# First layer's experts taken half by half, with each half's norm and query product moved among other work

## The chip, the cores and the metric

The kernel runs on one core of one Trainium2 chip. A core has a matrix engine (TensorE, PE in the profile), a vector engine (VectorE, DVE), an activation engine (ScalarE, ACT), a general engine (GpSimd, POOL) and a sync engine (SyncE, SP), which here only issues DMAs. Each runs its own instruction stream in order; they meet at semaphores. The metric is the time of one execution on the device, in microseconds (us); less is better.

## What is computed

Four layers on x, 8 batches of 128 tokens with 128 features, all in float32. Every layer is a cross attention and a mixture of experts (or feed forward), each behind a layer norm. Cut to what the change touches:

```python
x = x + tanh(g_xattn[0]) * L0_xattn(layernorm(x), ctx)
x = x + tanh(g_ffn[0]) * L0_ffn(layernorm(x))      # 8 experts, top 2, + 1 shared of double width
x = x + tanh(g_xattn[1]) * L1_xattn(layernorm(x), ctx, ctx, mask, Wq, bq)
x = x + tanh(g_ffn[1]) * L1_ffn(layernorm(x))      # own norm with gain; 8 experts, some "specialists"
# ... layers 2 and 3

def L0_ffn(x):      # w: softmax of x @ gate_w.T, top 2, normalised
    y = sum(w[:, e] * ((silu(x @ wg[e]) * (x @ wu[e])) @ wd[e]) for e in range(8))
    return y + (silu(x @ swg) * (x @ swu)) @ swd

def L1_xattn(q, k, v, mask, Wq, bq):      # 16 heads of 8, 77 keys per batch
    s = heads(q @ Wq.T + bq) @ heads(k).T / sqrt(8)
    return softmax(where(mask == 0, min, s)) @ heads(v)
```

## The kernel before

The 1024 tokens are two halves of 512 (HALF), four batches each (TH = 4). X is the residual stream with tokens in partitions, XN its normed form, XT (with its parts XTh and XTl) the normed form turned, with features in partitions. PS[0] to PS[7] are the eight PSUM banks. A float32 product is made of three matmuls (`mm3`) on a high and a low part of each operand. So every weight is split first: a "strip" is a cast on DVE to WH (`high_part`, L936) and then a subtraction on POOL to WL (`low_part`, L607). Weights arrive by DMA in RAW.

*The plan.* `plan()` writes the order of a mixture's steps by hand; PE, ACT, DVE and POOL each walk the same list ORDER[layer] in `mixture` and do their part of each step. For the first layer there are five units (E0P = 5): unit 0 is the shared expert, units 1 to 4 are pairs of experts. A step n of the list interleaves (`weave`) three things for successive pairs (unit, half): "gate_up" of x[n] (eight products into banks, Silu on ACT, product with the routing weight on DVE into SN), "turn0" of x[n-1] (SN turned, split in hidden parts H1h/H1l or H2h/H2l) and "down0" of x[n-2], which adds to bank PS[4 + half]. In before x runs (unit 0, half 0), (unit 0, half 1), (unit 1, half 0) and so on, so both halves' sums are complete only at the end. The strips of the next unit come with every second step. "route" parts 0 to 4 are the routing on DVE.

*Between experts and attention.* ACT copies the sums out of PS[4] and PS[5] into XT; PE turns them back (`turn_back`, L1538); DVE adds them to X (`summed`, L1103) and takes moments (`stats`, L891 to L900); POOL takes the power -1/2 (`rstd`, L600); DVE scales (`scaled`, L910); PE turns XN (`turn`, L1386); ACT copies to XT; PE multiplies with Wq; ACT adds the bias and writes the queries QT. POOL builds the key blocks BDK (`head_keys`, L640), two batches ahead; BDK lies over SN. Sixteen `keep_clock` matmuls on constants fill PE meanwhile.

*The attention.* `attention` runs on four engines, 32 iterations of one group of four heads (NG = 4 groups per batch), with lags: in iteration i PE makes the scores of group i in PS[i % 3] (L1366, BDK and a mask matmul MB), the transposes of group i-3 in PS[3 + g % 3] (L1563), and the values of group i-5 in PS[6 + batch % 2]. DVE takes the maximum of i (L1144) and subtracts it for i-1 (L1152), ACT the exponential (L769). The transposed groups are copied out by ACT, every fourth by DVE (L1157). For a finished batch DVE weighs the result (L1163 to L1177), for the first four of them followed by a "bias row" (three instructions for the specialists' biases). From iteration 22 on DVE also does half 0's two norms of the next mixture (`first_half_normed`). Half 1's follow behind the attention, and the step "second" turns them and computes the router's logits.

*The second mixture* starts with the four "up" products of expert 0, half 0, then "second", then four "spec0" tiles of 13 matmuls, each with its norm, woven with half 1's "up".

## Time and profile before

| | |
|---|---|
| median of three runs | 790.73 us (788.05 to 791.43) |
| span of the profiled execution | 791.2 us |
| PE busy | 700.5 us, 89% |
| DVE busy | 553.0 us, 70% |
| mean granted clock of PE | 0.922 |
| first layer's experts, on PE | 34.4 to 115.8 us |
| second attention, on PE | 131.5 to 200 us |

The span is the time from the first to the last instruction of one execution; durations of instructions come from that execution. A granted clock of 1.00 is 2.4 GHz, of 0.5 is 1.2 GHz; a stretch in between shows both. A busy PE may be doing keep-clock matmuls, which compute nothing. Rows give the start and the duration in us, and in brackets how long the engine was idle before and what released it.

### The profile page before, as it was taken

Reading aid. Unit: us, or ns where it says so; the run is one execution under the profiler, and the core shown is the slowest. Engines: PE = TensorE matmul, PEld = TensorE weight load, DVE = VectorE, ACT = ScalarE, POOL = GpSimd, SP = SyncE. Lnnn points to the kernel's source line nnn. Section 1 sums busy time; section 2 is a strip of 40 time slices with the busy share of each in tenths; the row PEclk is TensorE's granted clock in tenths of the full one; section 3 lists DMA queues with packets and bytes.
Section 4 is the critical chain, followed back from the end, with each engine's and each line's share of the span. In section 5 each row is a group of like instructions: output and inputs, shape, how many; then the busy total and the mean of one; then the engine's idle time right before and its main releaser. Section 6 shows DMA issues by size and latency. Waiting matters only on the chain.

```text
span 791.2 us, 10027 instructions
## 1 busy us (share of the span) xinstructions
PE 700.5 (89%) x3468; PEld 547.8 (69%) x3475; DVE 553.0 (70%) x1242; ACT 367.5 (46%) x647; POOL 209.9 (27%) x193
## 2 busy tenths in 40 slices
PE   5989997999898998797999797993759999789997
PEld 2779983889666766675777586771546888567775
DVE  4688766788578585656667735769874554588996
ACT  2334442434435737455275464721214442486673
POOL 5113107322132041124424311143002220214431
PEclk9589997999799999999999989986879999799999
DMA  5102003000001010202010200030000000001000
GB/s 134 39 27 58 2 4 114 31 1 1 1 14 67 3 38 1 68 0 80 14 68 14 66 1 0 1 97 0 1 0 1 1 1 1 27 27 28 1 1 27
DMA packets 27361, 20.97 MB, mean 27 GB/s; under 512 B 5409, under 2 KB 22571, under 8 KB 27311
## 3 DMA queue, kind: packets, MB, share of 16 engines
q1 hardware_dynamic: 26591, 20.29, 8.7%
q8 instruction: 28, 0.46, 0.3%
q14 instruction: 22, 0.18, 0.1%
q10 hardware_dynamic: 720, 0.04, 0.1%
HBM read 19.80 MB, written 0.52 MB: 26 GB/s over the span
## 4 chain that ended last, share of the span: by engine, by line
PE 70%; DVE 17%; issue 4%; ACT 4%; POOL 3%; DMA 1%; ACTq 0%; DVEq 0%; POOLq 0%
PE PS L1366 61%; PE PS L1563 4%; DVE H2l L1082 2%; PE PS L1448 2%; POOL WL L607 2%; ACT H1h L752 1%; DVE SN L1038 1%; PE PS L1499 1%; ACT G L750 1%; DVE WH L936 1%; DVE XN L910 1%; PE PS L1386 1%; DMA GW<-in_L_gate_T 1%; DVE ST L891 1%; POOL RSTD L617 1%
## 5 line engine op out<-in xcount | busy, mean ns | idle before, releaser
L607 POOL TENSOR_TENSOR WL<-RAW,WH 128x512 fp32r<-128x512 f32 (+2 forms) x76 | 95.4, 1272 | 186.9 <-DVE WH L936 186.9
L1082 DVE TENSOR_TENSOR H2l<-G,H2h 128x512 fp32r<-128x512 f32 x104 | 84.0, 822 | 59.7 <-ACT H2h L752 58.7
L1082 DVE TENSOR_TENSOR H1l<-G,H1h 128x512 fp32r<-128x512 f32 x80 | 63.3, 800 | 28.9 <-ACT H1h L752 28.1
L1366 PE MATMUL PS<-H1h,WH 128*128 128x512 f32 x146 | 60.9, 417 | 8.0 <-DVE H1l L1082 8.0
L750 ACT ACTIVATE G<-PS,UB 128x512 f32<-128x512 f32 x64 | 44.8, 700 | 42.4 <-PE PS L1366 38.1
L1366 PE MATMUL PS<-XTh,WH 128*128 128x512 f32 x128 | 55.3, 432 | 9.8 <-POOL WL L607 5.3
L600 POOL TENSOR_TENSOR RSTD<-VE,MHALF 128x4 f32<-128x4 f32 x18 | 19.3, 1072 | 166.5 <-DVE VE L900 166.5
L1366 PEld LDWEIGHTS PS<-V,ATT 77*128 77x128 f32 x512 | 62.5, 192 | 0.6
L625 POOL TENSOR_TENSOR XT<-XT,YW 128x512 f32<-128x512 f32 x24 | 34.8, 1448 | 106.0 <-DVE YW L1017 106.0
L769 ACT ACTIVATE ATT<-ATT 128x308 f32<-128x308 f32 x64 | 29.4, 460 | 71.3 <-DVE ATT L1152 71.0
L1366 PE MATMUL PS<-V,ATT 77*128 77x9 f32 x512 | 61.3, 247 | 0.0
L1144 DVE TENSOR_REDUCE MX<-PS 128x4 f32<-128x308 f32 x64 | 30.5, 477 | 43.6 <-PE PS L1366 42.9
L1366 PE MATMUL PS<-H1l,WH 128*128 128x512 f32 x146 | 58.6, 401 | 0.0
L1366 PE MATMUL PS<-H1h,WL 128*128 128x512 f32 x146 | 58.4, 400 | 0.0
L1366 PE MATMUL PS<-H2h,WH 128*128 128x512 f32 (+1 forms) x108 | 50.6, 469 | 5.6 <-issue 2.0
L1366 PE MATMUL PS<-XTl,WH 128*128 128x512 f32 x128 | 54.0, 422 | 0.0
L685 ACT ACTIVATE ATT<-PS 77x512 f32<-77x512 f32 (+5 forms) x76 | 38.2, 517 | 33.6 <-PE PS L1734 17.0
L1366 PE MATMUL PS<-XTh,WL 128*128 128x512 f32 x128 | 53.8, 420 | 0.0
L1366 PE MATMUL PS<-BDK,ATT 128*128 128x308 f32 x128 | 49.1, 466 | 1.6 <-issue 1.6
L750 ACT ACTIVATE G<-PS,FB 128x512 f32<-128x512 f32 x64 | 43.3, 698 | 13.9 <-PE PS L1366 13.8
L1366 PE MATMUL PS<-H2h,WL 128*128 128x512 f32 (+1 forms) x108 | 44.0, 408 | 0.0
L1366 PE MATMUL PS<-H2l,WH 128*128 128x512 f32 (+1 forms) x108 | 44.0, 407 | 0.0
(242 smaller groups left out, 1677.8 us busy)
## 6 DMA issues: line engine op xcount, KB each, us to landing
RAW<-in_L_ffn_spec_W SPq DMA_DIRECT2D x4, 1024.0 KB, 5.6
RAW<-in_L_ffn_w SPq DMA_DIRECT2D x16, 256.0 KB, 3.0
RAW<-in_L_ffn_up_W SPq DMA_DIRECT2D x8, 256.0 KB, 2.7
RAW<-in_L_ffn_down_W SPq DMA_DIRECT2D x8, 256.0 KB, 3.6
RAW<-in_L_ffn_spec1a_W SPq DMA_DIRECT2D x2, 512.0 KB, 4.3
RAW<-in_L_ffn_spec1b_W SPq DMA_DIRECT2D x2, 512.0 KB, 5.2
RAW<-in_L_ffn_wg SPq DMA_DIRECT2D x4, 176.0 KB, 2.7
RAW<-in_L_ffn_wu SPq DMA_DIRECT2D x4, 176.0 KB, 2.7
```

Source lines behind the costliest of these rows:

```text
L600: g.tensor_tensor(RSTD[:, c], VE[:, c], MHALF[:, c], ALU.pow).then_inc(rstd_ready, 1)
L607: g.tensor_tensor(lo, RAW[0:r["rows"], r["raw"] + s["c0"]:r["raw"] + s["c1"]], hi.bitcast(fp32), ALU.subtract).then_inc(lo_done, 1)
L617: g.tensor_tensor(RSTD[:, i:i + 1], VE[:, i:i + 1], MHALF[:, 0:1], ALU.pow).then_inc(trstd_ready, 1)
L625: g.tensor_tensor(y, y, YW[:, (d % 2) * HALF:(d % 2 + 1) * HALF], ALU.add).then_inc(y_added, 1)
L685: return s.activation(o, i, ACT.Copy)
L750: last = s.activation(G[:, k % 4, :], bank[:, :], func, bias=bias, scale=scale)
L769: s.activation(group(PB, g), group(SUB, g), ACT.Exp, scale=scale).then_inc(exp_done, 1)
L1082: v.tensor_tensor(lo, full, hi.bitcast(fp32), ALU.subtract).then_inc(split_done, 1)
L1144: v.tensor_reduce(MX[:, (g % 4) * GH:(g % 4 + 1) * GH], bank(g), AX.X, ALU.max).then_inc(max_done, 1)
L1366: return t_.matmul(o, l, r, start=start, stop=stop)
L1448: last = t_.transpose(o[0:rows, t * S:(t + 1) * S], SN[:, h, at:at + rows], ident[:, :])
L1563: last = t_.transpose(PS[3 + g % 3][0:KC, m * S:(m + 1) * S], group(PB, g)[:, m * KC:(m + 1) * KC], ident[:, :])
```

## The change

1. In the first layer x becomes (0,0), (0,1), then units 1 to 4 of half 0, then units 1 to 4 of half 1. Strips of units 1 to 4 come in steps 0 to 3, one unit per step. SN is used by step (slot n % 2), no longer by half.
2. Half 0's sum is complete at the end of step 7. Its copy, turning back, sum, moments, scaling, turn, Wq product and bias are steps of their own (the kinds in HELD) between the pieces of steps 7 to 10, in bank PS[4].
3. Half 1's same chain stands inside the second attention: PE's parts in iterations 1, 9 and 12 (`second_half`), DVE's in 2, 3, 4 and 6 (`second_half_normed`), ACT's in 8 and 10, in bank PS[5]. The attention's transposes therefore have two banks instead of three, in both attentions that use the function. QT, SUB and PB lie elsewhere, and the queries of half 1 are waited for at batch 4.
4. The six strips before the second mixture (`prepare(1)`) move on DVE from ahead of the attention to its iterations 10 to 15, on POOL from ahead of the third key block to behind the fifth. POOL's first key block waits for the last hidden split.
5. Half 0's turn for the second mixture stands in the attention's iteration 34. Half 1's two norms stand between the "up" splits, and two specialist tiles ahead of "second". Ring banks 6 and 7 wait for the attention's last outputs. The fourth layer's mixture turns half 1 in PS[5] too.
6. The turning back, the 16 keep-clock matmuls and the turns ahead of the attention are gone.

```diff
-    x = [(p, h) for p in range(E0P) for h in range(2)]
+    x = [(0, 0), (0, 1)] + [(p, h) for h in range(2) for p in range(1, E0P)]
...
-        more = strips(n // 2 + 1) if n % 2 == 0 and n // 2 + 1 < E0P else []
+        more = strips(n + 1) if n + 1 < E0P else []
...
+        elif n == E0P + 2:
+            order[0] += weave(a, b, c) + chain("y_copy")
+        elif n == E0P + 3:
+            u = weave(a, b, c)
+            order[0] += u[:3] + chain("y_back") + u[3:6] + chain("y_sum") + u[6:8] + chain("y_stats") + u[8:]
+        elif n == E0P + 4:
+            u = weave(a, b, c)
+            order[0] += u[:4] + chain("y_scale") + u[4:8] + chain("x_turn", "x_copy") + u[8:]
+        elif n == E0P + 5:
+            u = weave(a, b, c)
+            order[0] += u[:2] + chain("q_up", "q_copy") + u[2:]
...
-    o += up(0, 0) + second
+    u, s = up(0, 0), group("spec0", 1, 0, 0, TH)
+    o += u[0:1] + chain("late_scale") + u[1:2] + chain("late_stats") + u[2:4] + chain("late_norm") + s[0:2] + second
...
-            rstd(4, 5)
+            rstd(4)
+            pool.wait_ge(split_done, LAST0["hid"])
             head_keys(1, CT, range(2))
+            rstd(5)
+            head_keys(1, CT, range(2, TH + 1))
             prepare(1)
-            head_keys(1, CT, range(2, B - 1))
+            head_keys(1, CT, range(TH + 1, B - 1))
...
+                    if not first and i == 8:
+                        turned(2, halves=(1,), bank=PS[5])
+                    if not first and i == 10:
+                        queries(1, PS[5])
+                    if not first and i == B * NG + 1:
+                        turned(3, split=True, affine=True, halves=(0,), bank=PS[5])
...
+            def second_half_normed(i):
+
+                if i == 2:
+                    y0_summed(1, PS[5])
+                elif i == 3:
+                    moments(1, X)
+                elif i == 4:
+                    variances(2, 1)
+                elif i == 6:
+                    scaled(2, 1, X, XN)
+                elif 10 <= i < 10 + len(BEFORE[1]):
+                    high_part(BEFORE[1][i - 10])
...
-            norm(2, X, XN, summed(0))
-            prepare(1)
             attention(0, 1)
 
+            low_of_xt(1, (0,))
             stats(3, 1, X)
-            low_of_xt(1, (0,))
-            scaled(3, 1, X, XN)
-            dve.wait_ge(xn_ready, TH * (NORM_STEP[3, 1] + 1))
-            stats(4, 1, XN)
-            scaled(4, 1, XN, XM)
-            now(stream_plus_norm(1))
             mixture(1, 1)
...
-                    if g - g0 >= 3:
-                        pe.wait_ge(*copied_out(g - 3))
+                    if g - g0 >= 2:
+                        pe.wait_ge(*copied_out(g - 2))
                     for m in range(GH):
-                        last = t_.transpose(PS[3 + g % 3][0:KC, m * S:(m + 1) * S],
+                        last = t_.transpose(PS[3 + g % 2][0:KC, m * S:(m + 1) * S],
...
+            def second_half(i):
+
+                if i == 1:
+                    y0_back(1, PS[5])
+                elif i == 9:
+                    turn(2, *normed(2, XN), halves=(1,), bank=PS[5])
+                elif i == 12:
+                    queries(1, PS[5])
+                elif i == B * NG + 2:
+                    turn(3, *normed(4, XM), halves=(0,), bank=PS[5])
...
-            pe.wait_ge(split_done, LAST0["hid"])
-            turn_back(0)
-
-            keep_clock(16)
-            turn(2, *normed(2, XN))
```

PE from the last expert product to the first scores of the attention, before (XT,WQ are the query products, BDK the key blocks):

```order
L1366 MATMUL PS<-H1l,WH 128x512
L1366 MATMUL PS<-H1h,WL 128x512
L1538 MATMUL PS<-ident,XT 128x128 x8
L1366 MATMUL PS<-MB,identb 128x512 x16
L1386 MATMUL PS<-ident,XN 128x128 x8
L1366 MATMUL PS<-XT,WQ 128x512 x2
L1366 MATMUL PS<-BDK,ATT 128x308
```

and the same place of the changed kernel:

```order
L1422 MATMUL PS<-H1l,WH 128x512
L1422 MATMUL PS<-H1h,WL 128x512
L1422 MATMUL PS<-BDK,ATT 128x308
L1422 MATMUL PS<-MB,identb 128x308
L1422 MATMUL PS<-MB,identb 128x512 x3
L1451 MATMUL PS<-ident,XT 128x128 x4
L1422 MATMUL PS<-BDK,ATT 128x308
```

The scores now follow the last product directly, and half 1 is turned back behind the first of them.

POOL from the last strips of the first mixture through the attention, before (RSTD is the power, BDK a key block, WL a low part):

```order
L607 TENSOR_TENSOR WL<-RAW,WH 96x128
L600 TENSOR_TENSOR RSTD<-VE,MHALF 128x4 x2
L640 TENSOR_TENSOR BDK<-CT,HM 128x1232 x2
L607 TENSOR_TENSOR WL<-RAW,WH 128x512 x6
L640 TENSOR_TENSOR BDK<-CT,HM 128x1232 x5
```

and of the changed kernel:

```order
L622 TENSOR_TENSOR WL<-RAW,WH 96x128
L615 TENSOR_TENSOR RSTD<-VE,MHALF 128x4
L655 TENSOR_TENSOR BDK<-CT,HM 128x1232 x2
L615 TENSOR_TENSOR RSTD<-VE,MHALF 128x4
L655 TENSOR_TENSOR BDK<-CT,HM 128x1232 x3
L622 TENSOR_TENSOR WL<-RAW,WH 128x512 x6
L655 TENSOR_TENSOR BDK<-CT,HM 128x1232 x2
```

The six low parts moved from ahead of the third key block to behind the fifth, and half 1's power stands behind the second.

DVE behind the attention, changed kernel (XTl the low part of half 0, L922 to L931 moments of half 1, L1113 splits of the "up" results, L941 scalings, L1061 a tile's moments):

```order
L957 TENSOR_TENSOR XTl<-XT,XTh 128x512
L922 BN_STATS ST<-X 128x6 x4
L928 BN_AGGR MV<-ST 128x2 x4
L931 TENSOR_SCALAR VE<-MV 128x4
L1113 TENSOR_TENSOR H1l<-G,H1h 128x512
L941 TENSOR_SCALAR XN<-X,MV,RSTD 128x128 x4
L1113 TENSOR_TENSOR H1l<-G,H1h 128x512
L922 BN_STATS ST<-XN 128x6 x4
L928 BN_AGGR MV<-ST 128x2 x4
L931 TENSOR_SCALAR VE<-MV 128x4
L1113 TENSOR_TENSOR H1l<-G,H1h 128x512 x2
L941 TENSOR_SCALAR XM<-XN,MV,RSTD 128x128 x4
```

In before XTl stood behind the first moments, and the four splits in one row behind the whole norm chain.

## Rows read from the trace of the kernel before

**Rows 1.** Page: busy time of each engine; shares of the last chain.
```profile
PE 700.5 (89%) x3468; PEld 547.8 (69%) x3475; DVE 553.0 (70%) x1242; ACT 367.5 (46%) x647; POOL 209.9 (27%) x193
PE 70%; DVE 17%; issue 4%; ACT 4%; POOL 3%; DMA 1%; ACTq 0%; DVEq 0%; POOLq 0%
```
**Rows 2.** Stretches: length; busy PE, PEld, DVE, ACT, POOL; clock; DMA.
```profile
83.30:98.00 14.70, 14.70 (x94) 13.74 (x93) 11.75 (x27) 7.09 (x14) 3.05 (x4) 1.00 0.00 0
98.00:105.20 7.20, 7.20 (x48) 6.72 (x46) 4.74 (x12) 3.55 (x7) 0.00 (x0) 1.00 0.01 2
116.00:132.00 16.00, 10.60 (x35) 4.76 (x34) 12.15 (x34) 3.56 (x6) 11.32 (x7) 0.78 0.31 98
140.00:160.00 20.00, 20.00 (x153) 17.70 (x152) 14.24 (x36) 8.45 (x18) 4.92 (x3) 1.00 0.02 5
210.00:214.00 4.00, 4.00 (x13) 3.25 (x14) 2.35 (x4) 0.56 (x1) 0.00 (x0) 0.52 0.00 0
```
**Rows 3.** Timeline, experts to attention: start, duration, engine, line, instruction [idle before, releaser].
```profile
112.96 0.69 DVE L1075 TENSOR_TENSOR H1l<-PS,H1h 96x512 fp32r<-96x512 f32 x1 [0.28 <-ACT H1h L685]
...
115.40 0.39 PE L1366 MATMUL PS<-H1h,WL 96*128 96x512 f32 x1
...
118.39 0.69 DVE L1103 TENSOR_TENSOR X<-PS,X 128x512 f32<-128x512 f32 x1
...
120.51 6.24 DVE L910 TENSOR_SCALAR XN<-X,MV,RSTD 128x128 f32<-128x128 f32 x8
...
121.69 4.46 POOL L640 TENSOR_TENSOR BDK<-CT,HM 128x1232 f32<-128x1232 f32 x2
...
131.52 1.36 PE L1366 MATMUL PS<-BDK,ATT 128*128 128x308 f32 x2 [0.82 <-issue]
```
**Rows 4.** Timeline of PE, second attention: iterations 2 and 3, and later transposes.
```profile
135.93 0.68 PE L1366 MATMUL PS<-BDK,ATT 128*128 128x308 f32 x2
...
137.23 0.68 PE L1366 MATMUL PS<-BDK,ATT 128*128 128x308 f32 x2
...
161.92 0.60 PE L1563 MATMUL PS<-ident,ATT 128*77 128x128 f32 x4
```
**Rows 5.** PE: four transposes and what follows; last chain: two query products.
```profile
61.15 0.60 PE L1448 MATMUL PS<-ident,SN 128*128 128x128 f32 x4
61.50 0.41 PE L1366 MATMUL PS<-WH,XTh 128*128 128x352 f32 x1
...
597.03 1.93 PE PS L1366 x4
```
**Rows 6.** Slack in the attention; duration ns min/median/max of three kinds; POOL's low parts.
```profile
152.70 0.46 ACT L769 ACTIVATE ATT<-ATT 128x308 f32<-128x308 f32 x1 [2.65 <-DVE ATT L1152]
...
153.97 0.60 PE L1563 MATMUL PS<-ident,ATT 128*77 128x128 f32 x4
...
L910 DVE TENSOR_SCALAR XN<-X,MV,RSTD x8: 335/341/2286, 120.5 to 126.4; 128x128 f32<-128x128 f32 x8
...
L1167 DVE TENSOR_SCALAR RC<-RC,ANY x8: 233/233/1431, 149.3 to 199.8; 128x16 f32<-128x16 f32 x8
...
L936 DVE CAST WH<-RAW x22: 329/416/1032, 43.8 to 128.3; 128x352 fp32r<-128x352 f32 x8, 128x512 fp32r<-128x512 f32 x6, 128x256 fp32r<-128x256 f32 x4, 96x128 fp32r<-96x128 f32 x4
...
L607 POOL TENSOR_TENSOR WL<-RAW,WH 128x512 fp32r<-128x512 f32 (+2 forms) x76 | 95.4, 1272 | 186.9 <-DVE WH L936 186.9
```
**Rows 7.** Timeline: a copy by DVE, and the transposes two groups on.
```profile
190.87 0.68 DVE L1157 COPY ATT<-PS 77x512 f32<-77x512 f32 x1
...
192.94 0.64 PE L1563 MATMUL PS<-ident,ATT 128*77 128x128 f32 x4
```
**Rows 8.** Timeline of PE behind the attention: first "up", turn, second tile.
```profile
202.92 0.47 PE L1366 MATMUL PS<-XTh,WH 128*128 128x512 f32 x1 [2.60 <-DVE XTl L926]
...
207.84 1.10 PE L1386 MATMUL PS<-ident,XM 128*128 128x128 f32 x4 [0.34 <-DVE XM L910]
...
217.40 0.50 PE L1366 MATMUL PS<-ROWr,onesr 33*128 33x512 f32 x1
```

More of the change, by code:

```diff
@@ L360, in program @@
         K3T = ATT3[:, 2048:2048 + B * KC]
-        U0T = ATT[0:R0, 0:T]
+        U0T = ATT2[0:R0, 2048:2048 + T]
         VP0 = ATT3[0:R0, 0:B * KC]
@@ L685, in copy, with turned @@
                 return s.activation(o, i, ACT.Copy)
-            def turned(k, split=False, affine=False, halves=range(2)):
+            def turned(k, split=False, affine=False, halves=range(2), bank=None):
                 for h in halves:
+                    full = PS[6 + h] if bank is None else bank
                     act.wait_ge(xnt_full, 2 * k + h + 1)
@@ L693, in turned, with y0_out, queries @@
                         if affine:
-                            last = s.activation(d, PS[6 + h][:, :], ACT.Identity, scale=LNG[:, 0:1], bias=LNG[:, 1:2])
+                            last = s.activation(d, full[:, :], ACT.Identity, scale=LNG[:, 0:1], bias=LNG[:, 1:2])
                         else:
-                            last = copy(d, PS[6 + h][:, :])
+                            last = copy(d, full[:, :])
                         last.then_inc(ready, 1)
+            def y0_out(h):
+                act.wait_ge(y0_full, h + 1)
+                copy(XT[:, h * HALF:(h + 1) * HALF], PS[4 + h][:, :]).then_inc(y0_copied, 1)
+            def queries(h, bank):
+                act.wait_ge(in_small, SMALL_IN)
+                act.wait_ge(q_full, h + 1)
+                s.activation(QT[h], bank[:, :], ACT.Identity, bias=BQ1[:, 0:1]).then_inc(q_ready, 1)
             def mixture(n, layer):
@@ L708, in mixture @@
                     if kind == "second":
-                        turned(3 if layer == 1 else 7, split=True, affine=layer == 1, halves=(1,))
+                        turned(3 if layer == 1 else 7, split=True, affine=layer == 1, halves=(1,), bank=PS[5])
                         continue
@@ L804, in _ @@
             mixture(0, 0)
-            for i in range(2):
-                act.wait_ge(y0_full, i + 1)
-                copy(XT[:, i * HALF:(i + 1) * HALF], PS[4 + i][:, :]).then_inc(y0_copied, 1)
-            turned(2)
-            act.wait_ge(in_small, SMALL_IN)
-            for i in range(2):
-                act.wait_ge(q_full, i + 1)
-                s.activation(QT[:, i * HALF:(i + 1) * HALF], PS[i][:, :], ACT.Identity, bias=BQ1[:, 0:1]).then_inc(q_ready, 1)
+            y0_out(1)
             attention(0, float(DK) ** -0.5)
-            turned(3, split=True, affine=True, halves=(0,))
             mixture(1, 1)
@@ L1091, in mixture @@
                         weigh(s)
+                    elif kind == "y_sum":
+                        y0_summed(0, PS[4])
+                    elif kind == "y_stats":
+                        stats(2, 0, X)
+                    elif kind == "y_scale":
+                        scaled(2, 0, X, XN)
+                    elif kind == "late_scale":
+                        scaled(3, 1, X, XN)
+                    elif kind == "late_stats":
+                        dve.wait_ge(xn_ready, TH * (NORM_STEP[3, 1] + 1))
+                        stats(4, 1, XN)
+                    elif kind == "late_norm":
+                        scaled(4, 1, XN, XM)
+                        now(stream_plus_norm(1))
                     for m in ready:
@@ L1378, in keep_clock, with turn @@
                     mm(bank[:, :], identb[:, :], MB1[:, 0:HALF])
-            def turn(k, src, ready, halves=range(2)):
+            def turn(k, src, ready, halves=range(2), bank=None):
                 for h in halves:
+                    full = PS[6 + h] if bank is None else bank
                     for t in range(TH):
@@ L1385, in turn, with y0_back, queries @@
                         ready(i)
-                        last = t_.transpose(PS[6 + h][:, t * S:(t + 1) * S], src(i), ident[:, :])
+                        last = t_.transpose(full[:, t * S:(t + 1) * S], src(i), ident[:, :])
                     last.then_inc(xnt_full, 1)
+            def y0_back(h, bank):
+                pe.wait_ge(y0_copied, h + 1)
+                for t in range(TH):
+                    at = h * HALF + t * S
+                    last = t_.transpose(bank[:, t * D:(t + 1) * D], XT[:, at:at + S], ident[:, :])
+                last.then_inc(y_turned, 1)
+            def queries(h, bank):
+                pe.wait_ge(in_small, SMALL_IN)
+                pe.wait_ge(xt_ready, 4 + h + 1)
+                mm(bank[:, :], WQ1[:, :], XT[:, h * HALF:(h + 1) * HALF]).then_inc(q_full, 1)
             def normed(n, buf):
@@ L1411, in mixture @@
                     kind = s["kind"]
-                    if kind in ("split", "quantise", "route", "weigh"):
+                    if kind in ("split", "quantise", "route", "weigh") or kind in HELD:
+                        if kind == "y_back":
+                            y0_back(0, PS[4])
+                        elif kind == "x_turn":
+                            turn(2, *normed(2, XN), halves=(0,), bank=PS[4])
+                        elif kind == "q_up":
+                            queries(0, PS[4])
                         continue
@@ L1447, in mixture @@
                             at = t * 2 * I0 + i * 128
-                            last = t_.transpose(o[0:rows, t * S:(t + 1) * S], SN[:, h, at:at + rows], ident[:, :])
+                            last = t_.transpose(o[0:rows, t * S:(t + 1) * S], SN[:, s["slot"], at:at + rows], ident[:, :])
                         last.then_inc(ring_full, 1)
@@ L1580, in attention @@
                 for i in range(B * NG + VALUE_LAG):
+                    if not first:
+                        second_half(i)
                     if i < B * NG:
```

61 lines of the change are left out of this document (35 added, 26 removed).

## The prediction

> **What bounds the kernel now.** I began with the busy table and the shares of the chain that ended last [rows 1]. TensorE (PE) is busy for 700.5 of 791.2 us and is 70% of that chain; VectorE (DVE) is 17%. So the time is PE's own work plus the places where PE waits, and I looked for those places in the table of stretches [rows 2]. In the first layer's experts PE is busy without a gap (14.70 of 14.70 and 7.20 of 7.20 us). From 116 to 132 it is busy for 10.60 of 16 us, and most of that is clock-keeping matmuls; in the second attention it is again busy for 20.00 of 20 us. Around 210 to 214 it is busy, but at a granted clock of 0.52. The change works on those two holes.
>
> **Hole one, 115.8 to 131.5 us.** The last expert matmul ends at 115.40 + 0.39 = 115.79, and the attention's first score matmul starts at 131.52 [rows 3]: 15.7 us. What PE must do there is small: four groups of four transposes and two Wq products. The rest is one chain through ACT, DVE and POOL: half 1's sum and moments (from 118.39 to 120.51, 2.1 us), power, scaling (eight instructions in 6.24 us), then the keys (two in 4.46 us) [rows 3].
>
> After the change this chain is done for half 0 during the last expert steps, and half 1's runs inside the attention. What is late next is the pair of key blocks. They overlay the buffer SN, so POOL now waits for the last hidden split, which ends at 112.96 + 0.69 = 113.65. One of two key blocks takes 4.46 / 2 = 2.23 us, so the first is there at 115.9, and with a semaphore's delay the scores start at about 116.1. Gain 131.5 - 116.1 = **15.4 us**, bounds 14.5 (the two keys count together in part) and 15.6.
>
> **Filling the attention's pipeline.** The first three iterations last from 131.52 to 137.23, 5.7 us, but the third of them, already at the higher clock, lasts only 137.23 - 135.93 = 1.30 us [rows 3, 4]. PE now comes there straight from the experts, where the clock is 1.00 [rows 2]. Three at 1.3 us and one group of four transposes are 4.25 us. Gain **1.3 us**, bounds 0 and 1.5.
>
> **What PE takes over.** The moved work stays PE's, now in stretches in which PE has no idle time. Four transposes cost 61.50 - 61.15 = 0.35 us, two products of 512 columns with a 128x128 weight 1.93 us, so 0.97 each [rows 5]. Experts: 2 x 0.35 + 0.97 = 1.7 us. Attention: turning the normed half and its Wq product, 0.35 + 0.97 = 1.3 us (its first group of transposes is counted above). Loss **3.0 us**; this one has no wide bounds. The moved keep-clock matmuls, sixteen of them, only filled a wait.
>
> **DVE in the experts.** Now the units' weights are prepared in four successive steps (the first two as DVE still routes) instead of every second step. Two neighbouring steps with one unit's strips between them have DVE busy for 11.75 us; a step without strips has 4.74 [rows 2]. One unit's strips therefore cost 11.75 - 2 x 4.74 = 2.3 us, and a step with all of them 7.0 us, against PE's 7.2 to 7.35 us per step (7.20, and 14.70 / 2). DVE also waits inside a step for ACT and PE, so a little of this will reach PE; the ring of six banks hides about the rest. The step which gets half 0's sum and moments rises by 2.1 us [rows 3] to 6.8. I take a loss of **1.9 us**, bounds 0 (all hidden) and 4.5 (each of the four loaded steps slips by about 1.1 us).
>
> **DVE and POOL in the attention.** The second attention is PE's at (161.92 - 153.97) / 4 = 1.99 us per iteration [rows 4, 6]. DVE was busy 14.24 of 20 us in its first part [rows 2]. It now also gets half 1's sum, moments and scaling (iterations 2 to 6: 2.1 us, and four scalings of 0.34) and six casts of weights (0.42 us each, iterations 10 to 15), and POOL its six low parts (1.3 us each) among the keys [rows 6]. How far may DVE fall behind? At the first bias row in before, the exponential starts at 152.70 and ends at 153.16, and the transposes which read it start at 153.97 [rows 6]: 0.8 us were left, and nothing was late. The six casts alone are 2.5 us, spread over iterations with some 1 us of free DVE time each, and so would be hidden.
>
> But the two engines also hold each other up. Of the eight scalings of hole one the median is 341 ns and the longest 2286 ns [rows 6], about one key block of POOL, and POOL's two key blocks ran from 121.69 to 126.15, in the middle of them [rows 3]. In the attention, DVE's tensor_scalar on 16 columns takes 233 ns in the median and 1431 ns once [rows 6]. In the new code the scaling in iteration 6 can meet the key block of batch 3 (up to 2.3 us), and the weighting, bias rows and casts of iterations 12 to 17 meet six low parts in a row (up to 1.3 us for each meeting). Against 0.8 to 2 us of slack I take a loss of **2.5 us**, bounds 0 and 6.
>
> The Trainium skill, SBUF — State Buffer, section "Who interferes with whom", says that a DVE copy, cast or tensor_scalar in its two-port mode and a GpSimd instruction exclude each other, and that the loser "fully blocks" until the other's instruction ends. The row of 2286 ns agrees with it. Counting casts by their busy time alone, as the paragraph on the six casts does, gives no loss; by the page's rule a third to a half of the meetings cost a whole POOL instruction, which would be the upper bound of 6 us.
>
> **Two transpose banks instead of three**, in both attentions. The transposes of group g now wait for the copy of group g-2. Late in the attention, where DVE is most loaded, DVE's copy ends at 190.87 + 0.68 = 191.55 and the transposes two groups on start at 192.94 [rows 7]: 1.4 us of slack, and the value matmuls right behind wait for that same copy in any case. Cost 0, bounds 0 and 1.
>
> **Hole two, 199.5 to 217.4 us.** Before, PE starts the third layer's first "up" matmuls at 202.92, after 2.60 us of waiting for XTl, because DVE first took half 1's moments [rows 8]. Now XTl comes first and XM's transposes are already done inside the attention: start at about 201.8 in the same time frame. Then, before, PE waits for half 1's two norms, turns at 207.84, computes the logits and one specialist tile, partly at a clock of 0.52 [rows 2], and reaches the second tile at 217.40 [rows 8]. After, two specialist tiles stand ahead of the turn. They wait for the four hidden splits, between which half 1's norm chain now stands. Following DVE with its own durations (0.69 per split [rows 3], four scalings of 0.34, about 1.4 us for moments, the sum and moments being 2.1) the fourth split ends near 209; the first tile ends near 209.8, the second near 212.9, turn and logits near 215.2. At that point before had still one tile to do, to about 220.5: 5.3 us. Two things take from it: PE has gaps between 204.6 and 209, so the clock may fall again as it did in before (up to 2.5 us), and the four "up" parts of half 1 now stand together behind the tiles, where ACT needs 1.3 us and PE 0.7 us each (1 to 2 us). Gain **3.5 us**, bounds 1 and 5.5.
>
> **The sum.** 15.4 + 1.3 - 3.0 - 1.9 - 2.5 + 3.5 = 12.8 us. The span of the profiled execution, 791.2 us, and the median of the three runs, 790.7 us, differ by 0.5 us, so I take the sum straight from the median: 790.7 - 12.8 = **777.9 us**. With all bounds bad: 14.5 + 0 - 3.0 - 4.5 - 6 - 1 + 1 = 1 us gained; with all good: 15.6 + 1.5 - 3.0 + 5.5 = 19.6 us.
>
> **The rivals.**
> *Everything is hidden* (chance 0.18): DVE's slack absorbs the moved work. Then the two DVE losses go and hole two gives 5: 15.4 + 1.3 - 3.0 + 5 = 18.7, so 772. For it speaks that in before DVE was 1 us late at each bias row and PE never waited; against it POOL's six low parts, which used to run before the attention.
> *DVE paces the first half of the attention* (0.20): the meetings with POOL pile up in iterations 6 to 18, experts' steps slip as well: losses of 4.5 and 6 in place of 1.9 and 2.5, so 784. For it: the rows of 1431 and 2286 ns; against: a meeting needs the two to coincide.
> *Half 1's query comes late* (0.03): the attention needs it from iteration 16, and the chain (scaled at 6, turned at 9, product at 12) has some 3 iterations, 6 us, to spare. Were that used up, each further microsecond is lost whole; 783.
> *Slower than before* (0.05): the two transpose banks. If DVE's copy in every fourth group were late for the transposes in both attentions, there are 16 such groups; from 1.4 us of extra lateness on, each further microsecond costs up to 16 us. To undo the gain of 12.8 and 4 more it takes 1.05 us per group, so copies 2.5 us later than now in each: 795. Against it: in the fourth layer's attention DVE has no added work at all.
>
> **How the numbers follow.** Forecast 777.9, chance 0.54, with its own range 773 to 782. The range that should hold 8 in 10 takes in the hidden case and the paced one without its far end: 770 to 785.5. About 0.5% is what a measurement of this kernel can tell from no change, 4.0 us, so faster means under 786.8: the forecast, the hidden case, the late query and nearly all of the paced case, 0.91. Same 0.04, slower 0.05.
>
> **What would show it.** Right: PE's first score matmul comes within 1 us of its last expert matmul; the granted clock is 1.00 in the first iterations; the second attention's 32 iterations last 64 us plus 1.3, with short PE gaps at iterations 7 to 9 and 13 to 17, and there DVE instructions of over 1 us beside POOL's. From the last value matmul to the end of the logits come two tiles. Wrong: PE gaps of over 1 us per step in the experts' first steps (my 1.9 too small), a start of the attention held by the keys for more than 1 us, gaps ahead of transposes whose releaser is a copy out of the banks, or a clock of 0.5 for over 5 us behind the attention.

## The result, and the profile after

The changed kernel takes 811.39 us (median of 4 runs, 806.08 to 812.71), the kernel before 791.08 us in the runs beside it (788.05 to 793.03). The ratio is 1.0234, with a 95% interval of 1.019 to 1.0279. That is 20 us slower, clear of the noise, where the prediction had 12.8 us faster, and it lies outside the range.

Ahead of everything else, the page of the profiled execution; its first line answers to the busy table of [rows 1], then the granted clock in 40 slices of 20.2 us, and the chain that ended last by engine:

```profile
span 808.8 us, 10006 instructions
PE 717.9 (89%) x3459; PEld 566.4 (70%) x3459; DVE 557.5 (69%) x1242; ACT 366.3 (45%) x647; POOL 208.3 (26%) x193
...
PEclk9689999955599998999999989987689999789999
...
PE 69%; DVE 19%; issue 4%; ACT 3%; POOL 3%; DMA 1%; ACTq 0%; DVEq 0%; POOLq 0%
```

PE is busy for 17.4 us more than before, about the whole 17.6 us by which the span grew, though it has no new work to speak of. The reason stands in the clock: three slices in a row, from about 162 to 222 us, are at 0.5. The table of stretches shows it on PE (stretch; stretch's length and PE's busy time; instructions, granted clock, DMA share, GB/s):

```profile
150.00:156.00 6.00, 6.00 (x47) 1.00 0.64 213
156.00:160.00 4.00, 0.74 (x8) 0.94 0.03 8
160.00:170.00 10.00, 10.00 (x38) 0.50 0.01 2
...
210.00:220.00 10.00, 10.00 (x44) 0.50 0.00 0
```

One gap of 3.26 us, and then 60 us in which PE never waits and runs at the lower of its two levels, 1.2 instead of 2.4 GHz. PE's timeline around the gap (as in [rows 3]: start, duration, instruction, idle before and releaser):

```profile
116.55 0.39 PE L1422 MATMUL PS<-H1h,WL 96*128 96x512 f32 x1
...
117.25 0.76 PE L1422 MATMUL PS<-BDK,ATT 128*128 128x308 f32 x2 [0.32 <-issue]
...
121.67 0.68 PE L1422 MATMUL PS<-BDK,ATT 128*128 128x308 f32 x2
...
154.59 0.76 PE L1422 MATMUL PS<-BDK,ATT 128*128 128x308 f32 x2
...
159.99 1.36 PE L1422 MATMUL PS<-BDK,ATT 128*128 128x308 f32 x2 [3.26 <-DVE ATT L1214]
...
163.82 1.38 PE L1422 MATMUL PS<-BDK,ATT 128*128 128x308 f32 x2
...
202.29 1.37 PE L1422 MATMUL PS<-BDK,ATT 128*128 128x308 f32 x2
...
221.37 0.76 PE L1422 MATMUL PS<-XTh,WH 128*128 128x512 f32 x1 [1.22 <-DVE XTl L957]
```

117.25 is the first iteration's score, 121.67 that of iteration 3, 154.59 of 19, 159.99 of 20, 202.29 of 31, the last; an iteration now takes 163.82 - 159.99 = 3.83 us. For comparison, the rows of the kernel before that mark the same points and are not yet in [rows 3, 4, 8]: first expert matmul, scores of iterations 19 and 31, and first and last scores of the fourth layer's attention.

```profile
34.38 0.64 PE L1366 MATMUL PS<-WH,XTh 128*128 128x352 f32 x1
...
167.14 0.77 PE L1366 MATMUL PS<-BDK,ATT 128*128 128x308 f32 x2
...
190.96 0.76 PE L1366 MATMUL PS<-BDK,ATT 128*128 128x308 f32 x2
...
599.70 0.76 PE L1366 MATMUL PS<-BDK,ATT 128*128 128x308 f32 x2 [0.73 <-issue]
657.40 0.77 PE L1366 MATMUL PS<-BDK,ATT 128*128 128x308 f32 x2
```

In the kernel after, the first expert matmul starts at 33.56, and the fourth layer's attention at 617.32, with its last scores at 675.05. So the 17.62 us (617.32 - 599.70) divide as follows; what comes later takes the same time in both.

| stage | before, us | after, us | difference |
|---|---|---|---|
| up to the first expert matmul | 34.38 | 33.56 | -0.82 |
| experts, to the end of their last matmul | 81.41 | 83.38 | +1.97 |
| hole one, to the first score | 15.73 | 0.31 | -15.42 |
| iterations 0 to 3 | 5.71 | 4.42 | -1.29 |
| iterations 3 to 19 | 29.91 | 32.92 | +3.01 |
| iteration 19 to 20, with the gap | 1.99 | 5.40 | +3.41 |
| iterations 20 to 31 | 21.83 | 42.30 | +20.47 |
| last score to first "up" | 11.96 | 19.08 | +7.12 |
| from there to the fourth layer's attention | 396.78 | 395.95 | -0.83 |

Who made the gap? DVE's difference (line 1214) released the scores of iteration 20: PE may not overwrite a score bank before DVE has subtracted the peaks in it, and the row names DVE as what ended the wait. What DVE and POOL did up to there:

```profile
152.37 2.24 POOL L655 TENSOR_TENSOR BDK<-CT,HM 128x1232 f32<-128x1232 f32 x1
...
152.81 1.84 DVE L1229 TENSOR_SCALAR RC<-RC,ANY 128x16 f32<-128x16 f32 x1
...
155.58 2.25 POOL L655 TENSOR_TENSOR BDK<-CT,HM 128x1232 f32<-128x1232 f32 x1 [0.96 <-PE PS L1422]
...
155.65 2.45 DVE L1322 CAST ROWr<-ROW 1x512 fp32r<-1x512 f32 x1
...
158.85 0.48 DVE L1206 TENSOR_REDUCE MX<-PS 128x4 f32<-128x308 f32 x1
```

Two small DVE instructions, 0.23 us alone [rows 6] and 0.42 alone, each lasted until POOL's key block had ended: to 154.65 where the block ended at 154.61, and to 158.10 where it ended at 157.83. That is 3.6 us at one place, and the next peak stands behind them. The Trainium skill, SBUF — State Buffer, section "Who interferes with whom", says that a DVE cast or tensor_scalar in its two-port mode and a GpSimd instruction exclude each other, and that the one that comes second is fully blocked until the first ends. Both rows agree: POOL's block had started first each time.

### The profile page after: what moved, and what is told of

It is laid out like the page before. It is cut to its first block, busy times and chain, and to the rows that moved or that the text cites. A ratio compares the mean times of both kernels' runs of the same rounds, so it can differ in the third digit from the quotient of the medians.

```text
span 808.8 us, 10006 instructions
## 1 busy us (share of the span) xinstructions
PE 717.9 (89%) x3459; PEld 566.4 (70%) x3459; DVE 557.5 (69%) x1242; ACT 366.3 (45%) x647; POOL 208.3 (26%) x193
## 4 chain that ended last, share of the span: by engine, by line
PE 69%; DVE 19%; issue 4%; ACT 3%; POOL 3%; DMA 1%; ACTq 0%; DVEq 0%; POOLq 0%
PE PS L1422 60%; PE PS L1643 4%; DVE H2l L1113 2%; PE PS L1528 2%; DVE WH L967 2%; POOL WL L622 2%; PE PS L1579 1%; DVE XN L941 1%; DVE SN L1069 1%; ACT H1h L786 1%; PE PS L1443 1%; ACT G L784 1%; DMA GW<-in_L_gate_T 1%; POOL RSTD L632 1%; DVE H1l L1113 1%
## 5 line engine op out<-in xcount | busy, mean ns | idle before, releaser
L1113 DVE TENSOR_TENSOR H2l<-G,H2h 128x512 fp32r<-128x512 f32 x104 | 84.0, 822 | 60.5 <-ACT H2h L786 59.5
L1113 DVE TENSOR_TENSOR H1l<-G,H1h 128x512 fp32r<-128x512 f32 x80 | 64.5, 814 | 29.7 <-ACT H1h L786 28.8
L1422 PEld LDWEIGHTS PS<-V,ATT 77*128 77x128 f32 x512 | 77.2, 229 | 1.0 <-issue 0.6
L1422 PE MATMUL PS<-V,ATT 77*128 77x9 f32 x512 | 74.2, 273 | 0.0
L1422 PE MATMUL PS<-BDK,ATT 128*128 128x308 f32 x128 | 55.3, 518 | 4.6 <-DVE ATT L1214 3.3
L1643 PEld LDWEIGHTS PS<-ident,ATT 128*77 128x77 f32 x256 | 37.7, 172 | 13.3 <-issue 12.3
L1643 PE MATMUL PS<-ident,ATT 128*77 128x128 f32 x256 | 45.6, 308 | 0.4 <-ACT ATT L703 0.3
```

Source lines behind the costliest of these rows:

```text
L1113: v.tensor_tensor(lo, full, hi.bitcast(fp32), ALU.subtract).then_inc(split_done, 1)
L1422: return t_.matmul(o, l, r, start=start, stop=stop)
L1643: last = t_.transpose(PS[3 + g % 2][0:KC, m * S:(m + 1) * S], group(PB, g)[:, m * KC:(m + 1) * KC], ident[:, :])
```

## The experiments

Theory A: PE's gap of 3.3 us sets off the lower clock, and the attention's own work, once there, does not bring it back. Theory B: the lower clock comes from something else that the change brought (the moved work, two transpose banks), and the gap is a by-stander.

### The gap filled, in the changed kernel

```
 second_half(i)
+if 17 <= i < 21:
+    keep_clock(4, PS[5])
```

> The changed kernel, with four clock-keeping matmuls of 512 columns (results unused, into the bank that the half-1 work has left) ahead of the scores of iterations 17, 18, 19 and 20 of the second attention, so 16 matmuls, worked out at the higher clock as about 3.4 us of PE work. They stand where PE waited 3.26 us for the late exponentials. Theory A (PE's gap of 3.3 us at iteration 20 set off the granted clock of 0.50 that lasts to the attention's end, and that is what costs): no gap of over 1 us, granted clock 1.00 from 160 us to the end of the attention, iterations of 1.99 us instead of 3.85, so 811.4 minus about 29 = 782 us (777 to 787). Theory B (the low clock comes from what the attention now holds, the moved work and two transpose banks, whatever PE's gaps): the clock falls all the same and the time is 811 to 815 us.

Measured: 782.96 us (782.34 to 785.78), ratio to before 0.9897 [0.9861, 0.9932]. Nothing was taken away but the gap; sixteen unused matmuls were added, and the kernel became 28.4 us faster than the change (811.39 - 782.96).

```profile
156.00:160.00 4.00, 4.00 (x29) 1.00 0.10 27
160.00:170.00 10.00, 10.00 (x77) 1.00 0.00 1
```

Theory A gave 777 to 787, theory B 811 to 815. B falls. Whether it was the missing gap or the added wide matmuls that held the clock, this run can't say; the next one adds no matmul.

### The DVE work taken away there, in the changed kernel

```
-if layer == 1 and g // NG - first < 4:
+if layer == 1 and g // NG - first < 2:
     bias_row(g // NG - first)
+if layer == 1 and i in (22, 30):
+    settle()
+if layer == 1 and i in (34, 36):
+    bias_row(2 + (i - 34) // 2)
```

> The changed kernel with the third and fourth bias row (five DVE instructions each with their waits, 1.6 to 3.3 us on DVE) moved from iterations 17 and 21 of the second attention to iterations 34 and 36, behind its last scores; nothing is added. Theory A: without the row of iteration 17 DVE's peaks and differences of iterations 18 and 19 come about 2.5 to 3 us earlier, PE's gap shrinks from 3.26 us to under 1 us, the clock stays at 1.00 and the time is 780 us (775 to 785). Theory B (the low clock does not hang on the gap): 808 to 813 us. If POOL's key blocks alone make the gap, it stays over 2 us and the time stays near 811 us as well, but with the gap to be seen.

Measured: 781.66 us (777.12 to 784.18), ratio 0.9854 [0.9805, 0.9903]. The weighting still meets a key block, but what follows it is no longer late enough to matter: PE's rows show no wait there, iteration 19 starts at 155.67 and the last at 179.50, 23.83 us for twelve, as in the kernel before (190.96 - 167.14 = 23.82).

```profile
153.89 1.84 DVE L1229 TENSOR_SCALAR RC<-RC,ANY 128x16 f32<-128x16 f32 x1
```
```profile
160.00:170.00 10.00, 10.00 (x77) 1.00 0.01 2
```

So in the steady attention the gap decides. At the attention's end it is not the only thing that does. In this execution the clock fell at 184.7 us with no wait of PE ahead of it. The last scores had gone at 179.50, and PE only had transposes, value products and the early turn of half 0 left. The rows are from its timeline and its table of stretches:

```profile
183.29 0.96 PE L1426 MATMUL PS<-V,ATT 77*128 77x9 f32 x8
...
185.59 1.71 PE L1426 MATMUL PS<-V,ATT 77*128 77x9 f32 x8
```
```profile
184.00:186.00 2.00, 2.00 (x14) 0.60 0.00 0
```

It is the same in two of the kernels below, the one with the short gap (at 194.0 us) and the one with the weights' preparation in its old place (at about 192). In the kernel before and in the one with the gap filled the clock was 1.00 through the same piece. No run was made on what decides there.

### The gap alone, in the kernel before

```
 if layer == 1 and g // NG - first < 4:
     bias_row(g // NG - first)
+    if g // NG - first == 2:
+        for _ in range(4):
+            bias_row_again(2)
```

> The kernel before, unchanged but for the third bias row being prepared four times more at iteration 17 of the second attention: about 6.4 us more on DVE at one place, which from DVE's slack there should leave PE a gap of 3 to 4.5 us, as the changed kernel has. Theory A (a gap of this length is enough, and the attention's own work does not bring the clock back): granted clock 0.50 from there to the attention's end, 791 + 4 + 23 to 30 = 818 to 825 us. Theory B (the moved work or the two banks are needed for it): only the gap's own 4 us, 793 to 797 us.

> The kernel before with the third bias row prepared two times more at iteration 17 of the second attention. With four times more PE waited 8.07 us there (one of the added instructions, 2.62 us instead of 0.68, met a key block), and one repetition is 1.6 us; so two fewer leave a gap of 2.9 us without a meeting and 4.9 us with one. Theory A (a PE gap of about 3 us is enough for the lower clock, which then stays): clock 0.50 until the attention's end, 791 + 3 + 28 = about 822 us (818 to 827). If such a gap is too short for it, 793 to 796 us.

> The same with one repetition: a gap of about 1.3 us, at most 3.2 us with a meeting. The 0.5 us gaps of the changed kernel left the clock at 1.00 and the 3.26 us gap did not; this one stands between. Theory A with a gap that is too short for the lower clock: 791 to 793.5 us at a clock of 1.00. If a gap of 1.3 us is enough: 815 to 822 us.

> The kernel before with the two casts of the third bias row repeated once at iteration 17 and the low part of that row left out of the repetition, so that the third layer gets a rougher bias there (the output differs a little for that). It adds about 0.9 us to DVE, with a meeting up to 2.9 us, where one whole repetition added 3.5 us and made a gap of 3.06 us. Expected gap 0.3 to 2.4 us. Theory A: if it is near the changed kernel's harmless 0.5 us, 791 to 792 us at a clock of 1.00; if it is over 2 us, the lower clock and 815 to 818 us.

PE's row behind the gap in each, with four repetitions, two, one, and the short one, which repeats the two casts and leaves out the subtraction; the last two are followed by a row of their table of stretches (the clock is the number behind the count):

```profile
175.10 1.36 PE L1378 MATMUL PS<-BDK,ATT 128*128 128x308 f32 x2 [8.07 <-DVE ATT L1152]
```
```profile
170.64 1.36 PE L1378 MATMUL PS<-BDK,ATT 128*128 128x308 f32 x2 [4.73 <-DVE ATT L1152]
```
```profile
172.30 1.02 PE L1378 MATMUL PS<-BDK,ATT 128*128 128x308 f32 x2 [3.06 <-DVE ATT L1152]
```
```profile
180.00:190.00 10.00, 10.00 (x40) 0.50 0.00 0
```
```profile
165.93 0.76 PE L1378 MATMUL PS<-BDK,ATT 128*128 128x308 f32 x2 [0.41 <-DVE ATT L1152]
```
```profile
165.00:170.00 5.00, 4.59 (x36) 1.00 0.01 2
```

The times are 828.9, 822.75, 818.01 and 793.74 us (one run each), beside medians of 790.29 to 791.5 for the kernel before. Gaps of 8.07, 4.73 and 3.06 us cost 37.9, 31.3 and 26.5 us; the gap of 0.41 us costs 3.5 (793.74 - 790.29), less than what a single run can tell (the kernel before ran from 788.48 to 795.49 beside it), and leaves the clock at 1.00 for the next 28 us. So the kernel before, with none of the moved work and three transpose banks, shows the same loss: the gap is sufficient. For the first gap I had reckoned 3 to 4.5 us, and the time of 828.9 lies above the 818 to 825 I expected, for the same reason as in the prediction: one of the repeated subtractions met a key block and took 2.62 us instead of 0.68, with four repetitions, with two and with one alike. The next two gaps came out as I expected for a repetition with such a meeting. The repetition without the subtraction stayed clear. With four repetitions:

```profile
166.30 2.62 DVE L1263 TENSOR_TENSOR ROWr<-ROW,ROWr 1x512 fp32r<-1x512 f32 x1
```

### Bringing the clock back

```
 second_half(i)
+if i == 22:
+    keep_clock(16, PS[5])      # second kernel: keep_clock(4, PS[5])
```

> The changed kernel with sixteen clock-keeping matmuls of 512 columns ahead of the scores of iteration 22, two iterations behind PE's gap of 3.26 us. At the lower clock they take about 6.8 us. If a dense stretch of wide matmuls brings the clock back where the attention's own small ones do not: clock 1.00 soon behind them, iterations of 1.99 us again from about 24 on, so about 15 to 18 us won for 3.4 to 6.8 us spent: 796 to 803 us. If the low clock holds whatever PE does: 815 to 818 us.

> The changed kernel with four clock-keeping matmuls of 512 columns ahead of the scores of iteration 22, where sixteen brought the clock back (792.7 us). Four take about 1.6 us at the lower clock. If a short dense piece is enough: clock 1.00 from about iteration 23 and 786 to 790 us. If it takes a longer one: the clock stays at 0.50 and the time is 811 to 814 us.

Both keep the gap of 3.26 us. PE's timeline with sixteen, then with four:

```profile
159.24 1.36 PE L1422 MATMUL PS<-BDK,ATT 128*128 128x308 f32 x2 [3.26 <-DVE ATT L1214]
...
166.92 6.32 PE L1422 MATMUL PS<-MB,identb 128*128 128x512 bf16 x16
173.07 0.68 PE L1422 MATMUL PS<-BDK,ATT 128*128 128x308 f32 x2
```
```profile
166.80 1.87 PE L1422 MATMUL PS<-MB,identb 128*128 128x512 bf16 x4
168.46 1.24 PE L1422 MATMUL PS<-BDK,ATT 128*128 128x308 f32 x2
...
171.62 0.77 PE L1422 MATMUL PS<-BDK,ATT 128*128 128x308 f32 x2
```

792.71 and 787.89 us, one run each. Behind both sixteen and four wide matmuls PE is back at 2.4 GHz, behind the four within the next iteration, and it stays there to the attention's last score. The four take 1.87 us, and the kernel is 23.5 us faster than the change (811.39 - 787.89). For the sixteen I had expected 796 to 803 us, too much; for the four I had left open whether they would do. The Trainium skill, TensorE: Matmul & The Clock Gate, in the part "The HAM clock gate", says that "the default state is throttled, and activity releases the throttle". These runs agree for the wide matmuls. For the attention's own work, in which the profile has PE busy for 10.00 of 10.00 us, the rows above show no release in 60 us; there the measurement decides.

### Undoing or reordering parts of the change

First, the weights' preparation back in its old place ahead of the attention:

```
 mixture(0, 0)
+prepare(1)                    # DVE: six casts
 attention(0, 1)
...
-elif 10 <= i < 10 + len(BEFORE[1]):
-    high_part(BEFORE[1][i - 10])
...
+prepare(1)                    # POOL: six low parts, behind key blocks 0, 1
 rstd(5)
-head_keys(1, CT, range(2, TH + 1))
-prepare(1)
-head_keys(1, CT, range(TH + 1, B - 1))
+head_keys(1, CT, range(2, B - 1))
```

> The changed kernel with one part of it undone: the preparing of the third layer's first weights (six DVE casts, six low parts on POOL) stands ahead of the attention again, as in the kernel before, instead of the casts in iterations 10 to 15 and the low parts between the key blocks. If DVE's and POOL's moved work made the lag at iteration 17 (theory A), the gap of 3.26 us is gone or under 1 us, the clock stays at 1.00, the attention starts up to 2.5 us later for the casts, and the time is 781 to 786 us. If half 1's norm chain in iterations 2 to 12 made the lag, or bias rows and key blocks meet as before, the gap of over 2 us stays and the time is 808 to 815 us.

Measured: 790.91 us (784.05 to 793.24, 10 runs), ratio 0.997 [0.9936, 1.0004]. The expectation of 781 to 786 us missed. The gap at iteration 20 is gone, as theory A had it, but there is a new one that neither side expected:

```profile
123.58 4.96 DVE L966 CAST WH<-RAW 128x512 fp32r<-128x512 f32 x5 [6.32 <-DMA RAW<-in_L_ffn_spec_W]
...
129.75 1.40 PE L1420 MATMUL PS<-BDK,ATT 128*128 128x308 f32 x2 [8.13 <-DVE ATT L1211]
...
134.04 0.68 PE L1420 MATMUL PS<-BDK,ATT 128*128 128x308 f32 x2
```

The second cast waits for a weight transfer, and the peaks are queued behind it on DVE. In the kernel before, the same casts start at 126.67, behind the scalings, while PE stands in hole one. Note the clock: after a gap of 8.13 us it is back 4.3 us later, without any help. The two iterations between 129.75 and 134.04 hold scores and transposes and no value products yet, while those behind the other gaps hold all three. The place and the length of the gap differ as well, and no run separates the three, so why it came back here stays open.

Second, only POOL's order:

```
 head_keys(1, CT, range(2, TH + 1))
-prepare(1)
-head_keys(1, CT, range(TH + 1, B - 1))
+for s in BEFORE[1][0:3]: low_part(s)
+head_keys(1, CT, range(TH + 1, TH + 2))
+for s in BEFORE[1][3:]: low_part(s)
+head_keys(1, CT, range(TH + 2, B - 1))
```

> The changed kernel with only POOL's order altered: after key block 4 come three of the six low parts, then key block 5, then the other three low parts, then key block 6 (the change has all six low parts ahead of key block 5, which so started at 152.37 us instead of some 149, and met DVE's weighting, 1.84 us instead of 0.23, while key block 6 met the bias row at 155.58, 2.45 us instead of 0.42). If these two meetings make the lag (theory A): at most low parts of 1.27 us are met, PE's gap is under 1.3 us, clock 1.00 and 780 to 784 us. If DVE's own load makes it, the gap stays near 3 us and the time near 811 us; then POOL's order only decides what is met.

Measured: 816.83 us, ratio 1.0331 [1.0285, 1.0377]: my expectation failed. The two meetings are gone (the weighting took 0.23 us, the bias row's cast 0.42), and a third took their place: key block 5, now earlier, meets a cast of a weight.

```profile
145.61 2.25 POOL L655 TENSOR_TENSOR BDK<-CT,HM 128x1232 f32<-128x1232 f32 x1 [2.11 <-PE PS L1426]
...
145.70 2.44 DVE L971 CAST WH<-RAW 128x512 fp32r<-128x512 f32 x1
...
149.01 1.37 PE L1426 MATMUL PS<-BDK,ATT 128*128 128x308 f32 x2 [2.25 <-issue]
```
```profile
150.00:155.00 5.00, 5.00 (x21) 0.50 0.47 164
```

A gap of 2.25 us was enough for the lower clock, and it came four iterations sooner (before the scores of iteration 16), so the loss is larger. DVE's slack was therefore not used up at iteration 17 only: among the casts, too, one meeting of 2 us with a key block reaches PE.

### A version that beats both

On top of the moved bias rows, keep-clock matmuls at the attention's end:

```
+if B * NG - 2 <= i < B * NG + 2:
+    keep_clock(2, PS[5])
...
-keep_clock(2, PS[1])
+keep_clock(2 if first or i < B * NG + 4 else 6, PS[1])
```

> The changed kernel with the third and fourth bias row at iterations 34 and 36, as before, and twelve clock-keeping matmuls of 512 columns more at the attention's end (two in each of iterations 30 to 33, ahead of the scores or transposes, and four more in the last iteration). Without them the clock fell to 0.50 at about 184 us and the third layer's first up matmul started at 194.14, 13.8 us behind the last scores; with bias rows in their old place it took 10.3 us. If the clock stays at 1.00 over the attention's end: 777 to 780 us. If the added matmuls only cost their time (2.6 us at the higher clock): 782 to 785 us.

Measured: 781.2 us (780.23 to 782.25), ratio 0.9844 [0.9798, 0.9889]. Against the 781.66 of the moved rows alone that is no difference, so my expectation of 777 to 780 missed, if barely; but the clock no longer falls at the attention's end, 1.3 us of waiting leaves it alone, and the last score to the first "up" takes 190.28 - 178.06 = 12.22 us instead of 194.14 - 179.50 = 14.64.

```profile
190.28 0.47 PE L1426 MATMUL PS<-XTh,WH 128*128 128x512 f32 x1 [1.31 <-DVE XTl L957]
```
```profile
190.00:200.00 10.00, 8.41 (x31) 1.00 0.01 2
```

Then the same remedy in the experts:

```
 # PE, after the first unit's first transposes
+if (e, h, i) == (0, 0, 0): keep_clock(12)
 # ahead of its second transposes
+if (e, h, i) == (0, 0, 1): keep_clock(4)
```

> The kernel of the run before (bias rows at iterations 34 and 36, twelve clock-keeping matmuls at the attention's end), and now sixteen more in the first layer's experts, where PE waits 2.62 us at 44.8 and 1.24 us at 47.3 for DVE and the clock falls there, as it does in every kernel here: twelve behind the first unit's first transposes and four ahead of its next ones. Theory A, put to another place: PE is busy through these waits (12 at 0.21 us are 2.6 us), the clock stays at 1.00 until 60 us, and the matmuls from 47 to 51 us, now 0.49 us each instead of 0.32, save 1.5 to 3 us: 778 to 780 us. If filled waits don't help in the experts, 781 to 784 us.

Measured: 778.0 us (773.13 to 783.12, 6 runs), ratio 0.9855 [0.9804, 0.9905], the same as without within the intervals. The median lies in the 778 to 780 that theory A gave, but the rows show that it is not for theory A's reason: the clock did stay at 1.00, and it brought nothing there. Rows without the sixteen, then with them:

```profile
44.77 0.43 PE L1426 MATMUL PS<-WH,XTh 128*128 128x352 f32 x1 [2.62 <-DVE SN L1098]
...
53.55 0.66 PE L1532 MATMUL PS<-ident,SN 128*128 128x128 f32 x4 [0.26 <-DVE SN L1098]
```
```profile
43.69 2.75 PE L1426 MATMUL PS<-MB,identb 128*128 128x512 bf16 x12
...
54.60 0.66 PE L1534 MATMUL PS<-ident,SN 128*128 128x128 f32 x4 [1.29 <-DVE SN L1098]
```

From the first expert matmul (32.80 and 33.88) to the transposes in question it is 20.75 us without and 20.72 us with the sixteen: PE ran faster to the next product of DVE and waited 1.29 us for it instead of 0.26. There DVE sets the pace, and a faster PE changes nothing.

## Why the prediction was wrong, point by point

- **Hole one.** Forecast 15.4, measured 15.42: the first score comes 0.31 us behind the last expert matmul, for the reason given. The last hidden split ends at 114.81, POOL's two key blocks run from 114.88 for 4.48 us, so the first is there at about 117.1, and the score starts at 117.25.
- **Filling the pipeline.** Forecast 1.3, measured 1.29. The agreement is in part luck: the terms named, 5.7 - 4.25, give 1.45, not 1.3. (A reading was wrong too, without effect on the sum: in hole one the keep-clock matmuls fill 3.4 us of PE's 10.60, not most of them.)
- **Experts.** Forecast a loss of 1.7 for PE's work and 1.9 for DVE; measured 1.97 in all. DVE's part was about 0.3, near the bound 0. From 54 us on PE was busy without a gap.
- **Attention up to iteration 19.** PE's moved work was forecast at 1.3 us; measured are 3.01, so, by difference, 1.7 for waits on DVE and POOL. With the bias rows moved it is much the same (155.67 - 122.74 = 32.93 from iteration 3 to 19, against 32.92), and it was the whole loss of the attention up to its last scores, since iterations 19 to 31 took 23.83 us there; 1.7 is under the forecast of 2.5.
- **Two transpose banks.** Forecast 0. The fourth layer's attention, which the change leaves alone but for them, takes 657.40 - 599.70 = 57.70 us before and 675.05 - 617.32 = 57.73 after. The rival "slower than before" named this mechanism; there it did nothing. So the outcome to which it gave 0.05 came about, by another cause.
- **The step that failed: DVE and POOL in the attention, loss 2.5 with bounds 0 and 6.** The waits themselves came to 1.7 + 3.4 = 5.1 us, inside the bounds, by the mechanism named and at the place named (weighting, bias rows and casts of iterations 12 to 17). The share by which the prediction reached its bound of 6 us, "a third to a half of the meetings", stands on no row and not in the Trainium skill, so that the sum fell inside says little for it. What was wrong is the price of a microsecond. I summed waits that could fall anywhere, as if each cost its own length, where 3.26 us of them in one piece cost 28.4 us (811.39 - 782.96, against a kernel that even pays some 3 us for its filling: iterations 16 to 20 take 161.95 - 148.92 = 13.03 us there, where five at 1.99 are 9.95). For a lower clock in the attention the sum had no term at all. The upper bound should have been: 5 us of waits, and if they come together, 2 us more for each iteration left. From iteration 20 that is 20.5 us, and some 7 at the end. It would have made "slower than before" the outcome of the paced rival, not of a remote one.
- **What was there to read.** The kernel before shows the lower clock twice behind the attention. It fell just after the wait of 2.60 us [rows 8], and PE ran at 0.50 from 204 to 206 us. The 0.52 of [rows 2], at 210 to 214, has no such wait ahead of it: PE had waited 0.34 us for the turn [rows 8] and 0.21 us for the router's logits, and was running these when it fell.

```profile
209.94 1.71 PE L1366 MATMUL PS<-RW,XT 128*128 128x8 f32 x8 [0.21 <-ACT XT L694]
```

I used both for hole two, where wide matmuls follow and the clock is back after some 3 to 6 us, and did not ask what it would be in a stage that consists of narrow ones. I listed "a clock of 0.5 for over 5 us" as a sign only for the stretch behind the attention.
- **Hole two.** Forecast 3.5, bounds 1 and 5.5. In the changed kernel it can't be read, since it starts at the lower clock. With the gap filled, the last score to the first "up" takes 11.22 us (193.03 - 181.81) against 11.96, and from there to the fourth layer's attention 396.11 against 396.78: 1.4 us. At a group of transposes of SN in the third layer the gain was still 2.4 us (236.29 - 181.81 = 54.48 from the last score, 247.84 - 190.96 = 56.88 before). About 1 us of it went in one wait behind that, for ACT's WGT, which is 2.13 us now and was 0.95 before. The size was wrong, the direction right.
- **The forecast's core.** With the gap filled or avoided the kernel takes 783 or 781.7 us, inside the range of 770 to 785.5 and 4 to 5 us above the forecast, of which hole two is 2.

## What to carry to other kernels

A wait on TensorE is not priced by its length alone. Before work is moved on to the engines that feed a long stretch of narrow matmuls, ask how long the longest single gap could be, and how much of the stretch lies behind it; here 2.25 to 3.3 us in one piece cost 26 to 34 us (26.5 for 3.06, 28.4 for 3.26, 816.83 - 782.96 = 33.9 for 2.25, which came earliest), and 0.4 us hardly anything. Where such a gap can't be excluded, a few wide matmuls in or behind it are a cheap insurance: four of them, 1.9 us, saved 23.5 us. In the experts, where DVE sets the pace, they brought nothing. Nor is the absence of a gap a guarantee: look at the granted clock also where the work gets light, as at the attention's end, where it fell in three kernels with no wait of PE ahead.

## What the runs showed of the hardware that I had not expected

- TensorE stayed at 0.50 of its clock for about 60 us and more (75 us in the kernel with POOL's order altered), to the attention's end, with no wait of over 0.23 us in the profile, in five kernels with a gap of 2.25 to 8.07 us inside the steady attention. Behind four bf16 matmuls of 512 columns it was back within one iteration.
- It also fell with no wait of over 0.1 us just ahead: at 184.7, 194.0 and about 192 us in three kernels, each at the end of the attention, where the scores are over.
- Behind a gap of 8.13 us at the attention's start, where scores and transposes run without value products, the clock came back in 4.3 us with no matmul added.
- Waits of 0.41 and 1.31 us left it at 1.00, the second with added wide matmuls ahead of it, and so did a wait of 1.79 us among the third layer's experts (at 236.29, in the kernel with the gap filled). A wait of 1.64 us at the end of the attention was followed by the lower clock (first "up" at 193.03 of 0.77 us, in that same kernel). So the length of a wait alone does not tell.
- Meetings of DVE and POOL repeat from kernel to kernel, where the order around them is the same: the same subtraction took 2.62 us in three, the same weighting 1.84 us in two (one profile each). So they can be found in a trace and moved, but moving one instruction can make the next one meet.
